# Routing counted in tiles, later loads of two experts, and another order in the token mixing

## The reference

```python
x = x + 0.5 * ffn(layernorm(x))      # f = 0
x = x + rwkv(layernorm(x))           # token mixing and channel mixing
x = x + 0.5 * ffn(layernorm(x))      # f = 1, the same weights

def ffn(x):                          # 16 heads, 4 key/value heads of 128
    h = x + causal_attention(rmsnorm(x))
    xt = rmsnorm(h)
    logits = xt @ gate_w             # 8 experts
    topv, topi = top_k(logits, 2)    # two choices per token
    p = softmax(topv)
    return h + sum over both choices of p * (silu(xt @ w1[e]) * (xt @ w3[e])) @ w2[e]

def rwkv(x):
    xln = ln(ln(x, ln1), tm)                       # second norm: time mixing
    mix = xln * time_first + shift(xln) * (1 - time_first)
    r = sigmoid(mix @ Wr)
    vmix = sum over t of (xln @ Wv)[t] * exp(time_decay * (T - 1 - t))
    x2 = x + r * (vmix @ Wo + bo)
    xc = ln(ln(x2, ln2), cm)
    return x2 + sigmoid(xc @ Wcr) * (square(relu(shift(xc) @ Wck)) @ Wcv)
```

## Time and profile before

| | us |
|---|---|
| median of three runs | 1265.64 (1265.47 to 1267.07) |
| the profiled execution | 1261.89 |
| its span, first to last instruction | 1260.1 |
| PE busy | 1158.2 (92%) |
| DVE busy | 941.4 (75%) |
| ACT busy | 800.5 (64%) |
| POOL busy | 568.7 (45%) |

### The profile page before, as it was taken

One profiled execution on the slowest core, in us unless ns is written; L12 is line 12 of the kernel. 1 busy time (PEld: TensorE's weight loads), 2 busy tenths in 40 slices (PEclk: granted clock), 3 DMA queues, 4 the chain that ended last, 5 costly groups with the idle time before them and its releaser, 6 DMA issues.

```text
span 1260.1 us, 18765 instructions
## 1 busy us (share of the span) xinstructions
PE 1158.2 (92%) x6520; PEld 972.9 (77%) x6520; DVE 941.4 (75%) x1998; ACT 800.5 (64%) x1575; POOL 568.7 (45%) x421
## 2 busy tenths in 40 slices
PE   4899999999999899992989789999999999889994
PEld 3788888888888478781669578888888888758883
DVE  6777887887887777667677777787787788677773
ACT  5666676666665377674555666666666666457773
POOL 3666666666620034430001375765775660015551
PEclk9999999999999999996989999999999999999997
DMA  4100100100015611242100200010010010741113
GB/s 136 38 1 1 39 1 1 38 1 1 2 51 194 232 39 54 68 143 76 55 1 1 71 1 1 2 38 1 5 34 1 1 51 1 261 174 55 50 52 121
DMA packets 45100, 65.90 MB, mean 52 GB/s; under 512 B 5840, under 2 KB 28368, under 8 KB 44880
## 3 DMA queue, kind: packets, MB, share of 16 engines
q1 hardware_dynamic: 40016, 50.55, 12.5%
q0 software_dynamic: 4416, 12.06, 3.1%
q10 hardware_dynamic: 576, 2.10, 0.4%
HBM read 54.47 MB, written 10.22 MB: 51 GB/s over the span
## 4 chain that ended last, share of the span: by engine, by line
PE 43%; DVE 5%; ACT 2%; issue 1%; POOL 1%; DMA 1%; SPq 0%; DVEq 0%; ACTq 0%; POOLq 0%
PE ps L1634 11%; PE ps L1636 10%; PE ps L1635 10%; PE ps L1704 5%; PE ps L1785 3%; PE ps L1773 1%; PE ps L1842 1%; DVE stats L1385 1%; PE ps L1615 0%; DVE h L1218 0%; DMA mixT<-y_dram 0%; PE ps L1756 0%; ACT probs L811 0%; DVE probs L1417 0%; DVE ps L1196 0%
## 5 line engine op out<-in xcount | busy, mean ns | idle before, releaser
L811 ACT ACTIVATE probs<-ps,negmax 128x128 f32<-128x128 f32 (+7 forms) x256 | 189.8, 742 | 89.2 <-DVE negmax L1196 86.0
L817 ACT ACTIVATE probsT<-ps 128x512 fp32r<-128x512 f32 x288 | 170.5, 598 | 110.3 <-PE ps L1704 108.6
L1202 DVE TENSOR_TENSOR probsT<-ps,probsT 128x512 fp32r<-128x512 f32 x288 | 196.0, 685 | 45.5 <-ACT probsT L817 44.1
L1196 DVE CUSTOM_DVE_ANT_0 ps<-ps,causal 128x128 f32<-128x128 f32 (+7 forms) x256 | 193.4, 761 | 28.0 <-PE ps L1636 26.3
L687 POOL TENSOR_TENSOR crossed<-crossed,rope 128x512 f32<-128x512 f32 x70 | 90.7, 1296 | 189.2 <-ACT crossed L797 189.1
L1704 PE MATMUL ps<-square,probs 128*128 128x128 f32 x1152 | 170.5, 273 | 5.7 <-ACT probs L811 5.3
L1704 PEld LDWEIGHTS ps<-square,probs 128*128 128x128 f32 x1152 | 141.0, 140 | 34.4 <-issue 4.2
L734 POOL DMA_INDIRECT xs<-rows_dram,token_of x46 | 68.8, 1496 | 182.4 <-DMA rows_dram<-probs 158.1
L1309 DVE TENSOR_TENSOR parts<-experts,parts 128x1024 fp32r<-128x1024 f32 x92 | 112.4, 1225 | 51.0 <-ACT parts L861 50.5
L1218 DVE SCALAR_TENSOR_TENSOR h<-ps,rowinv,h 128x256 f32<-128x256 f32 x256 | 123.5, 483 | 35.2 <-PE ps L1636 26.5
L1634 PE MATMUL ps<-keysT,queriesT 128*128 128x512 f32 (+4 forms) x384 | 141.6, 369 | 3.3 <-DVE straight L1172 1.4
(11 more groups left out here) (258 smaller groups left out, 2840.0 us busy)
## 6 DMA issues: line engine op xcount, KB each, us to landing
experts<-in_L_ffn_w_dram SPq DMA_DIRECT2D x48, 512.0 KB, 7.6
w_in<-in_L_ffn_wq_dram SPq DMA_DIRECT2D x8, 512.0 KB, 4.0
wo_in<-in_L_ffn_wo_dram SPq DMA_DIRECT2D x8, 512.0 KB, 5.9
rows_dram<-probs ACTq DMA_DIRECT2D x4, 512.0 KB, 7.2
probs<-y_dram SPq DMA_DIRECT2D x8, 256.0 KB, 4.4
mixT<-y_dram SPq DMA_DIRECT2D x8, 256.0 KB, 5.3
probs<-in_L_attn_x_dram SPq DMA_DIRECT2D x2, 512.0 KB, 5.2
w_in<-in_L_ffn_wk_dram SPq DMA_DIRECT2D x8, 128.0 KB, 4.7
```

Source lines behind the costliest of these rows:

```text
L811: act.activation(probs[:, i % 2, k, 0:w], ps[:, 2 * slot_n:2 * slot_n + 2, :].rearrange("p b n -> p (b n)")[:, at:at + w], ACT.Exp, bias=n ...
L817: act.activation(probsT[:, m % 3, 0, :], ps[:, 4 + m % 2, :], ACT.Copy).then_inc(S["probsT_high"], 1)
L1196: dve.tensor_tensor_reduce(out=row, in0=row, in1=causal[:, T - w:T], scale=-1.0, scalar=LARGEST, op0=ALU.add, op1=ALU.min, accum_out=negma ...
L1202: dve.tensor_tensor(probsT[:, m % 3, 1, :], ps[:, 4 + m % 2, :], probsT[:, m % 3, 0, :].bitcast(F32), ALU.subtract).then_inc(S["probsT_low ...
```

## The change

Routing counts in tiles instead of slots: the matrices of ones and of earlier partitions hold 1/128, so the counts and the slot come out of PE in tiles. Three DVE steps become unnecessary (two copies out of PSUM, the multiplication by 128), and the tile is found in one step instead of two. The number of the choice moves out of `marks` into the 16 `in_place` steps, as a second per-partition scalar with a second operation; `in_tile` disappears. Stored rows and results are numbered tile by tile (`(t p)`) instead of partition by partition (`(p t)`). Experts 3 and 4, and x behind them, are loaded after the first tile of gathered rows has been transposed. The six broadcast rows for the mixing are loaded one by one from tile 6 on instead of together at tile 13. `take_xs` signals each of its two chunks, and `up` waits for them one by one.

In the mixing, `bdW` moves behind `b1`; PE transposes each half in one go and does the decay products of both halves after the first, the second half's transposes behind them; chunk 1 of the shifted tokens is scaled by DVE instead of ACT; `low(0)` goes ahead of `centred`, two `add_h` go ahead of `gated_value(3)`, and `value(2)` goes ahead of `last_half(1)`. Fillers: 11 instead of 14 ahead of the picks, 54 ahead of the first transposes instead of 8 between the halves, 12 new ones ahead of the first `squares_in`.

```diff
-SPINS = (14, 18, 20, 8, 40)
+SPINS = (11, 18, 20, 54, 40, 12)
-    before = (r[:, None] < r[None, :]).astype(np.float32)
+    before = (r[:, None] < r[None, :]).astype(np.float32) / P
-    small[:, C_THR:C_THR + E * E] = np.tile(np.where(e == 0, -1, P * e), E)
+    small[:, C_THR:C_THR + E * E] = np.tile(np.where(e == 0, -1, e), E)
-    small[:, C_CHOICE:C_SPARE] = 1 + T * (choice // NT) + NT * r[:, None] + choice % NT
+    small[:, C_CHOICE:C_SPARE] = 1 + r[:, None] + P * np.arange(CHOICES)
-    small[:, C_PLACE:C_LEFT] = r[None, :]
+    small[:, C_PLACE:C_LEFT] = -r[None, :] / P
+    small[:, C_TILE:C_TILE + NS] = ROUND + np.arange(NS)
...
-        rows_tiles = rows_dram.rearrange("(p t) d -> p t d", t=NT)
-        y_choices = y_dram[0:TOPK * T].rearrange("(k p t) d -> k p t d", k=TOPK, t=NT)
+        rows_tiles = rows_dram.rearrange("(t p) d -> p t d", p=P)
+        y_choices = y_dram[0:TOPK * T].rearrange("(k t p) d -> k p t d", k=TOPK, p=P)
...
-                sp.wait_ge(S["ys_ready"], 13)
                 for n, name in enumerate(("ln1_g", "ln1_b", "ln2_g", "ln2_b", "bo", "time_decay")):
+                    sp.wait_ge(S["ys_ready"], 7 + n)
...
                 sp.wait_ge(S["pv_done"], NT * KVH * (f + 1))
-                for e in (2, 3, 4):
+                load_expert(2)
+                sp.wait_ge(S["xs_turned"], NS * f + 1)
+                for e in (3, 4):
                     load_expert(e)
...
                 for c in range(DC):
-                    last = act.activation(xsT[:, par, 0, c, :], ps[:, 4 + par, c * P:(c + 1) * P], ACT.Copy,
-                                          scale=cols[:, c, N2:N2 + 1])
-                last.then_inc(S["xsT_high"], 1)
+                    act.activation(xsT[:, par, 0, c, :], ps[:, 4 + par, c * P:(c + 1) * P], ACT.Copy,
+                                   scale=cols[:, c, N2:N2 + 1]).then_inc(S["xsT_high"], 1)
...
                 act.wait_ge(S["xT_edge"], 1)
-                act.wait_ge(S["xT_taken"], DC * (half + 1))
-                for c in range(DC):
-                    place = slice(half * HALF, (half + 1) * HALF)
-                    act.activation(mixT[:, c, place], xT[:, c, place], ACT.Copy, scale=keep[:, c:c + 1]).then_inc(S["mix_half"], 1)
+                act.wait_ge(S["xT_taken"], DC * half + 1)
+                act.activation(mixT[:, 0, place], xT[:, 0, place], ACT.Copy, scale=keep[:, 0:1]).then_inc(S["mix_half"], 1)
...
-            link(dve.memset(ones16[:], 1.0))
+            link(dve.memset(ones16[:], 1.0 / P))
...
-                link(dve.tensor_copy(logits[:], ps[:, 3, 0:NT * E].rearrange("p (t e) -> p t e", t=NT)))
+                logits = ps[:, 3, 0:NT * E].rearrange("p (t e) -> p t e", t=NT)
...
-                link(dve.tensor_copy(count[:], ps[:, 1, 128:128 + E]))
-                link(dve.tensor_tensor(sq, count[:].rearrange("p (e o) -> p e o", o=1).broadcast_to([P, E, E]),
+                link(dve.tensor_tensor(sq, ps[:, 1, 128:128 + E].rearrange("p (e o) -> p e o", o=1).broadcast_to([P, E, E]),
...
-                link(dve.tensor_scalar(count[:], first[:], float(P), None, ALU.mult))
...
-                link(dve.tensor_scalar(tilef[:], slotf[:], 1.0 / P, (1.0 - P) / (2 * P), ALU.mult, ALU.add))
-                link(dve.tensor_scalar(tilef[:], tilef[:], ROUND, ROUND, ALU.add, ALU.subtract))
-                link(dve.tensor_tensor(in_tile[:], small[:, C_SLOT:C_TOKEN].rearrange("p (o n e) -> p o n e", o=1, e=E)[:, :, :, 0]
-                                       .broadcast_to([P, CHOICES, NS]),
-                                       tilef[:].rearrange("p (c o) -> p c o", o=1).broadcast_to([P, CHOICES, NS]), ALU.is_equal))
-                link(dve.scalar_tensor_tensor(out=placef[:], in0=tilef[:], scalar=-float(P), in1=slotf[:],
-                                              op0=ALU.mult, op1=ALU.add))
-                dve.tensor_tensor(marks[:], in_tile[:], small[:, C_CHOICE:C_SPARE].rearrange("p (c o) -> p c o", o=1)
-                                  .broadcast_to([P, CHOICES, NS]), ALU.mult).then_inc(S["marked"], 1)
+                link(dve.tensor_scalar(tilef[:], slotf[:], (1.0 - P) / (2 * P), ROUND, ALU.add, ALU.add))
+                dve.tensor_tensor(marks[:], small[:, C_TILE:C_TILE + NS].rearrange("p (o n) -> p o n", o=1).broadcast_to([P, CHOICES, NS]),
+                                  tilef[:].rearrange("p (c o) -> p c o", o=1).broadcast_to([P, CHOICES, NS]), ALU.is_equal
+                                  ).then_inc(S["marked"], 1)
+                link(dve.scalar_tensor_tensor(out=placef[:], in0=tilef[:], scalar=ROUND, in1=slotf[:],
+                                              op0=ALU.subtract, op1=ALU.subtract))
                 for n in range(CHOICES):
-                    dve.tensor_scalar(in_place[:, n, :], place16[:], placef[:, n:n + 1], None, ALU.is_equal
-                                      ).then_inc(S["marked"], 1)
+                    dve.tensor_scalar(in_place[:, n, :], place16[:], placef[:, n:n + 1], small[:, C_CHOICE + n:C_CHOICE + n + 1],
+                                      ALU.is_equal, ALU.mult).then_inc(S["marked"], 1)
...
-                for c in range(DC):
-                    dve.wait_ge(S["mix_half"], DC * half + c + 1)
+                for c in (1, 0):
+                    dve.wait_ge(S["xT_taken"], DC * half + c + 1)
+                    if c == 0:
+                        dve.wait_ge(S["mix_half"], half + 1)
+                    else:
+                        link(dve.tensor_scalar(mixT[:, c, place], xT[:, c, place], keep[:, c:c + 1], None, ALU.mult))
...
                 combine(0, 0)
-                dve.wait_ge(S["decsum_ps"], 1)
-                for c in range(DC):
-                    dve.scalar_tensor_tensor(out=bdW[:, c, :], in0=ps[:, 2, 0:D], scalar=cols[:, c, TMB:TMB + 1], in1=Wv[:, c, :],
-                                             op0=ALU.mult, op1=ALU.mult)
                 outer_moments(0)
...
                 b1 = affine(OUTER, 1, 1, 1)
+                dve.wait_ge(S["decsum_ps"], 1)
+                for c in range(DC):
+                    dve.scalar_tensor_tensor(out=bdW[:, c, :], in0=ps[:, 2, 0:D], scalar=cols[:, c, TMB:TMB + 1], in1=Wv[:, c, :],
+                                             op0=ALU.mult, op1=ALU.mult)
...
+                low(0)
                 step = centred(INNER, h, 2, range(4, NT))
-                low(0)
                 squares(0)
...
                 gated_value(2)
-                gated_value(3)
                 add_h(2)
                 add_h(3)
+                gated_value(3)
                 squares(1)
...
-                pe.wait_ge(S["xsT_ready"], NS * f + tau + 1)
                 for k in range(2):
                     pe.wait_ge(S["w13_low"], 2 * (NS * f + tau) + k + 1)
                     for c in range(DC):
+                        if k == 0:
+                            pe.wait_ge(S["xsT_ready"], DC * (NS * f + tau) + c + 1)
...
-                first_half(0)
                 spin(SPINS[3], 3)
-                first_half(1).then_inc(S["m_done"], 1)
+                turn_half(0)
+                decayed(0)
+                decayed(1).then_inc(S["m_done"], 1)
+                turn_half(1)
                 gates(0)
...
                 pe.wait_ge(S["wk_low"], 5)
+                spin(SPINS[5], 0)
                 squares_in(0)
                 value(0)
                 value(1)
+                value(2)
                 pe.wait_ge(S["cr_sig"], 4)
                 last_half(1)
-                value(2)
                 value(3)
```

More of the change, by code:

```diff
@@ L269 @@
 C_LEFT = C_PLACE + P
-C_ALL = C_LEFT + NT
+C_TILE = C_LEFT + NT
+C_ALL = C_TILE + 24
 CHOICES = TOPK * NT
@@ L395, in macaron @@
             w2 = experts[:, :, 2 * DC * F:].rearrange("p e (c n) -> p e c n", c=FC)
-            logits = sb("logits", [P, NT, E], c=phase)
+            sb("routing_spare", [P, NT * E + E], c=phase)
             work = sb("work", [P, NT, E], c=phase)
@@ L402, in macaron @@
             wts = sb("wts", [P, 2, NT], c=phase)
-            count = sb("count", [P, E], c=phase)
             cube = sb("cube", [P, NS, E], c=phase)
@@ L418, in macaron @@
                 gated = sb("gated", [P, 2, F], c=tiles_phase)
-                in_tile = sb("in_tile", [P, CHOICES, NS], c=tiles_phase)
                 in_place = sb("in_place", [P, CHOICES, P], F16, c=tiles_phase)
@@ L1231, in route @@
                 dve.wait_ge(S["logits_ps"], f + 1)
-                link(dve.tensor_copy(logits[:], ps[:, 3, 0:NT * E].rearrange("p (t e) -> p t e", t=NT)))
+                logits = ps[:, 3, 0:NT * E].rearrange("p (t e) -> p t e", t=NT)
                 for k in range(TOPK):
-                    src = logits if k == 0 else work
+                    src = logits if k == 0 else work[:]
                     if k == 1:
@@ L1238, in route @@
                         dve.reciprocal(rstd[:, 0:1, :], std[:, 0:1, :]).then_inc(S["rstd_ready"], 1)
```

(15 more changed lines are left out.)

12 lines of the change are left out of this document (5 added, 7 removed).

## The result

The changed kernel takes 1245.3 us (median of 4 runs, 1243.17 to 1246.85); the kernel before, beside it, 1265.56 (4 runs, 1259.19 to 1267.07). The ratio is 0.9846, 95% interval 0.9818 to 0.9873: 16 to 23 us faster. The forecast was 1254.0 and 11.65 faster, its range 1249.5 to 1259.5. The sign was right, the gain was undersized, and the time lies outside the range. The profiled execution of the changed kernel took 1246.85 (span 1245.0), 15.1 less span than before. Two executions in a slow state are left out of all medians: one of e15 (5397.96) and one of the kernel before in the same group of runs (1697.38).

The account below looks back on a forecast made before the run. PE, busy 92% of the span, was taken as the bound, with time won at its waits, low clock and fillers. 2.2+5.0+3.7+0.75 = 11.65 off 1261.89 gave 1250.2, plus 3.75 made 1254.0; range 1249.5 to 1259.5.

Parts of the forecast that it names:

- The step that failed: Expert tiles: issuing the six `rows` loads one a tile touches no wait, gain 0.
- rival 4: Routing: expert loads get ahead of a gather and stall PE, 6.4 us a routing, 12.8 slower, 1266.8; chance 0.03.
- Mixing, first half: Mixing up to the decay groups' end: reordering and 54 fillers gain net 5.0 us, bounds 4.0 and 6.2.
- the 1.27 of the next item: Mixing, second half: low(0) starts 1.5 us earlier, the 12 fillers take 0.2 of it, leaving 1.27.
- Mixing, second half: Earlier low(0) and kept clock in squares_in(0) gain 3.7 us; value(2) ahead of last_half(1) adds 0.75.
- Routing: Both routing stretches with their first expert tiles: 2 x 0.80 + 0.63 = 2.2 us gained.
- The fillers ahead of `pick_ready`, 11 instead of 14, cost 0: Routing: changing the number of first fillers costs nothing, because PE waits there anyway.
- the 0.80 of the forecast: Routing, DVE chain: 1.75 us of steps removed less 0.90 and 0.05 for the second scalar, each routing.
- rival 1: Routing: the clock holds, 20 fillers take 4.4 us, 3.2 more gained over both, 1250.8; chance 0.28.
- The second scalar: Routing: a second per-partition scalar lengthens each of 16 `in_place` steps by 0.056 us, 0.90 in all.
- The first tile: First expert tile of each routing: chunk signals let PE start sooner, 0.63 us for both, bounds 0 and 1.2.
- The level: Whole kernel: the median lies 3.75 us above the profiled execution, so 1250.2 becomes 1254.0.

Follow-up runs that it names:

- e15: The kernel before with one edit: DVE reads the gate logits in PSUM instead of copying them first; 1265.5 us.
- e1: The kernel before with one edit: the six broadcast rows loaded one by one from tile 6 on; 1260.22 us, ratio 0.9969.
- e2: The changed kernel with the six broadcast rows loaded together at tile 13 again; 1248.51 us, ratio 0.988.
- e4: The kernel before with only the routing, loads, row layout, chunk signals and 11 first fillers; rows loads together, mixing as before; 1263.05 us, ratio 0.9999.
- e7: The changed kernel with one signal a tile from ACT and DVE instead of one a chunk; 1246.39 us, ratio 0.9863.
- e10: The changed kernel with choice numbers multiplied into `marks` by an extra DVE step, so `in_place` has one scalar again; 1241.6 us, ratio 0.9833.
- e16: The kernel before with only the routing, loads, row layout and chunk signals changed, but the copy of the logits kept; 1261.0 us.
- e5: The changed kernel with 14 fillers instead of 11 ahead of the choice counts; 1245.5 us.
- e9: The changed kernel with fillers that multiply their own tile of 1.0 instead of the 1/128 tile; 1245.0 us.

## Why the prediction was right in sign and wrong in size

- **The step that failed**: "The six `rows` loads, now one a tile from tile 6 on instead of together, touch no wait of the trace: 0." It rests on "In the expert tiles PE runs without a gap", and that was false at 524.68. e1 shows it: the edit alone is worth 3.0 us by medians (1263.22 to 1260.22; 2.0 to 5.7). e2 shows it from the other side in its profile, where the wait is back; its median, 1248.51, is 3 above the changed kernel's, but in another group, and the intervals of the two ratios overlap. In the profiles the stall costs 2.9 to 6.0, in the one at hand 5.0: PE waited 2.4 for a gather that moved beside 0.8 MB of other loads, some 0.9 was lost besides (as in e2 to e4, where the clock stayed), and the clock took the other 1.6. Loads that hold up a gather are the mechanism of rival 4, which I priced for the new kernel and did not look for in the old: "The trace of before has no gather beside a long load" passed over the one at 516.73.
- **Mixing, first half** (5.0): right, by its steps. The first normalised tile comes 2.78 earlier (2.8), DVE's product behind the last decay group 6.03 (5.9), the low clock behind 3.5 idle us as taken. squares_in(0) starts 6.8 earlier, for 6.3 with the 1.27 of the next item.
- **Mixing, second half** (3.7 with 1.27 of it ahead): squares_in(0) 14.22 us to the next product for 16.91, -2.7 for -2.5; behind it -1.0 for -0.75. In all 10.45 for 9.45. The profiled execution of before was also a quick one here: 118.7, and 118.6 to 121.9 in four other kernels with the old mixing (mean of five 120.2), against 109.0 on average in ten with the new and 54 fillers. So the typical gain is 11.2, mis-sized by 1.8: 1.0 between the two profiles, by the small terms above, and 0.8 since the sum was made from one lucky execution.
- **Expert tiles**: 5.153 us each for 5.187, 1.5 us over 44 tiles, not foreseen. At f=1 the second and third of each three products last 389 and 394 ns on average, for 395 and 397. e7 and e10 have it, e15 doesn't, e16 has it: not the signals, not PSUM, not `in_tile`; what remains (row layout, loads, where the tensors lie) was not separated.
- **Routing** (2.2): 2.0 in the profiles (0.45+1.55), but not by its steps. "The fillers ahead of `pick_ready`, 11 instead of 14, cost 0" held for their number (e5), not for the stretch: the counts came 0.7 late by the clock. Where the first fillers keep it (e9, both stretches), `token_of` comes 10.9 us behind the first read for 11.7, the 0.80 of the forecast. What the fall took, f=1's 20 fillers at the full clock gave back (rival 1, in one stretch). The second scalar, with its operation, was as charged (0.061 for 0.056). The Trainium skill's tier table (VectorE: DVE Perf Modes, The perf-mode tier table) names no charge for it; by that alone the 16 steps would have stayed at 2.69, and the trace has 3.66. The first tile gave 2 x 0.2 (6.02 for 6.22), not 0.63.
- **Rival 4** in the new kernel: no PE wait for a DMA in tiles 2 to 4 in any profile. The loads do slow the gathers beside them: the two at 440.94 and 444.89 land 6.2 and 5.8 us after their issue, where before they took 2.8 and 2.7, and at f=1 one takes 7.7. All three landed 1.6 us or more before PE used them, so nothing waited. The Trainium skill (DMA: Bandwidth & Descriptors, Queues, rings and completion order) has each DMA engine take turns between queues. The trace agrees: the first of them landed at 447.1, and behind all 4 MB it would have been 452.5, the estimate of rival 4. But taking turns is not free, as the 7.9 us of the gather at 516.73 show.
- **The level**: the profiled execution of before was 3.75 under the median, and I carried that over unchanged. Part of it was a quick attention(1), 407.04 against 408.0 to 411.0 in the other kernels. With averages over the kernels, 4.1 of stall, 11.2 for mixing, and 2.0 for routing and 1.4 for tiles from the one pair of profiles make 18.7 of the 20.3 measured. So of the 8.6 us of gain that the forecast missed, the stall is 4.1, mixing 1.8, the tiles 1.4, routing -0.2; some 1.5 stay open. As single edits they don't add up as well: e4's interval allows 2 us at most for routing and tiles, e16's 0.5 to 5.4; this is left as it is.

## What to carry to other kernels

Before a moved load is costed at nothing, list every PE wait on a DMA in the stretch where it stood, one by one: a stall of 2 us in 115 doesn't show in a busy share. Here it cost 1.4 to 1.5 times its length where the clock stayed, and 2 to 2.6 times where it fell behind. Make the sum against several executions or several kernels that share a stage, since one profile can be lucky by the size of the terms. Where the clock falls in nearly every execution, ask not whether filler keeps it but where the fall is cheapest: filler that ends ahead of the next wait, and short filler between thin matmuls.

## What the hardware showed that I had not expected

The granted clock is not a function of the program alone: the same instructions hold 1.00 in one execution and fall to 0.50 in another (11 fillers in 2.54 and 4.22 us). Most falls cost 1.7 us of PE time (4.22 for 2.53, 6.16 for 4.48, 5.73 for 4.04), wherever they come; the longest among the first fillers cost 2.3 (5.51 for 3.18, e15). A second per-partition scalar with its operation costs 0.061 us on a 128x128 f16 step; such steps follow each other 0.168 apart without it. Loads of 0.8 MB in all kept a gather from landing for 7.9 us, though the DMA engines were busy for only 0.54 to 0.68 of the time. And the second of three equal matmuls of 512 columns takes 389 or 395 ns on average, kernel by kernel.
